# Scan stage: the order in which ScalarE's copy of u B reads PSUM and writes SBUF

## The reference, cut to what matters

```
dA  = exp(dt_t[:, :, None] * A)
hst = hst * dA + (dt_t * x_t)[:, :, None] * B_t[:, None, :]
y_t = einsum('bds,bs->bd', hst, C_t)
```

## Time and profile before

| what | us |
|---|---|
| median of three runs | 9105.0 |
| the profiled execution | 9109.74 |
| its span, first to last instruction | 9107.9 |
| stretch of the scan stage from the first to the last scan | 1341 to 6057 |
| VectorE busy in it (2048 scans) | 4616.65 |
| ScalarE busy in it | 4356.62 |
| TensorE busy in it | 4024.19 |

### The profile page before, as it was taken

One profiled execution on the slowest core, in us unless ns is written; L12 is line 12 of the kernel. 1 busy time (PEld: TensorE's weight loads), 2 busy tenths in 40 slices (PEclk: granted clock), 3 DMA queues, 4 the chain that ended last, 5 costly groups with the idle time before them and its releaser, 6 DMA issues. The chain is left out here.

```text
span 9107.9 us, 235238 instructions
## 1 busy us (share of the span) xinstructions
PE 7455.4 (82%) x94416; PEld 3961.6 (43%) x94416; DVE 6331.0 (70%) x5563; ACT 5948.1 (65%) x8010; POOL 1341.5 (15%) x799
## 2 busy tenths in 40 slices
PE   7677758888888888888888888877688888888888
PEld 4333324444444444444444444442244444344444
DVE  1332339999999999999999999963245344354554
ACT  1333339999999999999999999951135334343544
POOL 0000003222222222222222222310000000000000
PEclk8787769999899898889998999988899999999999
DMA  4444442222222222222222222223200000000000
GB/s 143 98 97 98 102 97 67 65 65 67 65 64 67 67 65 65 67 65 65 66 65 65 67 65 65 69 99 129 99 5 5 7 7 5 16 20 10 7 8 10
DMA packets 621391, 541.98 MB, mean 60 GB/s; under 512 B 490256, under 2 KB 528784, under 8 KB 606736
## 3 DMA queue, kind: packets, MB, share of 16 engines
q1 hardware_dynamic: 620320, 527.39, 19.8%
HBM read 381.77 MB, written 145.49 MB: 58 GB/s over the span
## 5 line engine op out<-in xcount | busy, mean ns | idle before, releaser
L1086 DVE TENSOR_TENSOR_SCAN s_h<-s_decay,s_h 128x1040 f32<-128x1040 f32 x2048 | 4616.6, 2323 | 132.2 <-ACT s_decay L1010 127.4
L981 ACT COPY s_h<-s_pb 128x1024 f32<-128x1024 f32 x2048 | 2514.3, 1228 | 190.9 <-PE s_pb L912 163.3
L925 PE MATMUL s_py<-s_h,s_cz 128*32 128x128 f32 x32768 | 2516.1, 437 | 1.7 <-DVE s_h L1086 1.7
L1010 ACT ACTIVATE s_decay<-s_pa 128x1024 f32<-128x1024 f32 x2048 | 2179.6, 1065 | 60.3 <-issue 55.0
L897 PE MATMUL s_pa<-s_dl,s_al 18*128 18x64 bf16 x32768 | 908.2, 198 | 666.9 <-ACT s_decay L1010 568.3
L925 PEld LDWEIGHTS s_py<-s_h,s_cz 128*32 128x32 f32 x32768 | 1056.3, 127 | 459.2 <-issue 4.7
L897 PEld LDWEIGHTS s_pa<-s_dl,s_al 18*128 18x128 bf16 x32768 | 660.7, 99 | 988.7 <-ACT s_decay L1010 912.8
L912 PEld LDWEIGHTS s_pb<-s_ul,s_bl 18*128 18x128 bf16 x16384 | 492.3, 97 | 1077.4 <-ACT s_h L981 866.1
L912 PE MATMUL s_pb<-s_ul,s_bl 18*128 18x128 bf16 x16384 | 867.6, 228 | 75.4 <-issue 59.1
L1053 POOL TENSOR_TENSOR s_h<-s_h,s_one 128x64 f32<-128x64 f32 x384 | 696.6, 1814 | 725.9 <-DVE s_h L1086 725.9
L1041 POOL TENSOR_TENSOR s_cz<-s_cl,s_one 128x128 f32<-128x128 f32 x256 | 320.4, 1252 | 2746.6 <-PE s_py L925 2734.3
(11 more groups left out here) (206 smaller groups left out, 6630.7 us busy)
## 6 DMA issues: line engine op xcount, KB each, us to landing
s_bl<-B SPq DMA_DIRECT2D x1024, 72.0 KB
s_ul<-U SPq DMA_DIRECT2D x1024, 72.0 KB
s_dl<-D SPq DMA_DIRECT2D x1024, 72.0 KB
s_al<-A SPq DMA_DIRECT2D x256, 144.0 KB
D<-p_dp SPq DMA_DIRECT2D x64, 384.0 KB, 6.5
U<-p_up SPq DMA_DIRECT2D x64, 384.0 KB, 5.3
B<-p_bz SPq DMA_DIRECT2D x144, 128.0 KB, 2.5
SZ<-p_sz SPq DMA_DIRECT2D x16, 1024.0 KB, 3.9
```

The costliest lines, as they stand in the source:

```text
L925: mm = pe.matmul(py[e % 2][QR * q:QR * q + QR, 0:P], cz[e % 2][:, l * P + QR * q:l * P + QR * q + QR], states, start=(l == 0), stop=(l == ...
L981: act.copy(out, pb[:].rearrange("p b t d -> p d b t")).then_inc(bu_done, 1)
L1010: act.activation(decay[(STEPS * e + 2 * z + j) % RING][:, :, 1:W], pa[j % 2][:], ACT.Exp).then_inc(exp_done, 1)
L1086: dve.tensor_tensor_scan(seg, decay[(STEPS * e + 2 * z + j) % RING][:].rearrange("p d w -> p (d w)"), seg, 0.0, ALU.mult, ALU.add).then_in ...
```

## The change

`take_bu` copies the same 1024 values of each partition from the same PSUM tile to the same places of `hb`, with the same waits and the same semaphore. Only the order in which it goes through them is another.

Before, the copy went channel by channel: for each of the 128 rows of `hb` it read 8 values of `pb`, each 128 values (512 bytes) behind the one before, and wrote them as two runs of 4 adjacent values. After, it goes time by time: for each of the 8 times it reads the 128 channels, which are adjacent in `pb`, and writes them one to a row, each 65 values (260 bytes) behind the one before.

```
-                    out = hb[at][:, :, 1:W].rearrange("p d (g a i) -> p d g a i", g=Q, i=4)[
-                        :, :, 2 * (h % 2):2 * (h % 2) + 2, h // 2, :]
-                    act.copy(out, pb[:].rearrange("p b t d -> p d b t")).then_inc(bu_done, 1)
+                    out = hb[at][:, :, 1:W].rearrange("p d (g a i) -> p g a i d", g=Q, i=4)[
+                        :, 2 * (h % 2):2 * (h % 2) + 2, h // 2]
+                    act.copy(out, pb[:]).then_inc(bu_done, 1)
```

## The result

The changed kernel takes 10,442.15 us (median of four runs, 10,438.45 to 10,451.34) against 9106.47 us: the ratio is 1.147, with a 95% interval of 1.145 to 1.149. It is 1336 us slower. The forecast was 950 us slower and a range up to 10,350 us. The direction and the new bound came out, the size did not. The profiled execution takes 10,442.36 us, its span is 10,440.6 us.

What follows compares the result with a forecast made beforehand. VectorE bounds the scan stage now; ScalarE at 2.70 us a step would make 21.9 us a tile, a stage of 5660 us against 4716 (+944), plus 6 for first copies: +950 on 9109.7, so 10,060 us, range 9020 to 10,350.

Steps and rivals of the forecast that it cites:

- the new bound: In the scan stage ScalarE, at 2.70 us a step, would replace VectorE, at 2.254 us a scan, as the bound.
- the reads are free: In the copy of `pb`, removing the separate PSUM reads would gain nothing; the old copy's 122 ns belonged to its writes.
- a value alone in its group of four: In the copy's writes to `hb`, each value alone in its aligned group of four costs 0.832 to 0.95 ns extra.
- L987 no longer waits: The small copy L987 would lose its 0.60 us wait for `ch` in each tile.
- The sign that the prediction had named for a wrong sum: First copies at 1.9 us while the scan stage still isn't near 5660 us.
- per step: ScalarE's step in the scan stage: copy slot 1.79 us plus exponential 0.91 us, 2.70 us, with TensorE done in time.
- The gaps at the loop's ends: ScalarE's gaps in front of exponentials that nothing released, 55.0 us at 17 places, would stay.
- the row for 0.95 ns a lone value: The old copy's 122 ns over 128 lone values, 0.95 ns each, would make the new copy 1.98 us.
- the round number of one slot: Each lone value in the copy costs one more slot of 0.832 ns, making the new copy 1.88 us.
- the clock in `ch`: TensorE's lower clock could show in `ch`; nothing was added for it, but the top of the range held it.
- reading (b): Copy's writes to `hb`: lone values in aligned groups of four cost extra; 10,060 us, own range 9900 to 10,350, chance 0.56.

Runs made afterwards that it cites:

- `ch_adj_after`: The changed kernel with TensorE's `ch` reading an adjacent 128-value tile instead of the states (y left out); 10,275 us.
- `bu_thin`: The changed kernel with `bu` making 2 of its 8 matmuls a step after the first tile; 10,418 us.
- `probe`: The kernel before, plus extra ScalarE and VectorE copies and memsets in many patterns, run in the quiet before the first tile; 9159.26 us.

## Why the prediction was wrong

Right were: the bound passes from VectorE to ScalarE in this stage; the reads are free; a value alone in its group of four is what costs; L987 no longer waits. The direction followed from these. The sign that the prediction had named for a wrong sum came: the first copies were near 1.9 us (1.97), and the stage took 6035 us and not 5660.

The step that failed is the term "per step": a slot of 1.79 us for the copy, 0.91 for the exponential, and nothing added for what TensorE does beside them. Per tile the mean distances of starts in the changed kernel's trace are 8 x 0.994 from an exponential to its copy, 6 x 1.900 + 1.967 + 1.894 for the copies, 0.178 + 0.212 for the small ones: 23.60 us, gaps included, against 21.9 + 0.2 in the forecast. By these slots the 375 us between 5660 and 6035 us of the stage come from:

- TensorE's single reads beside ScalarE's single writes: 1.878 instead of 1.79 us at 2040 copies, 180 us. The stage of `ch_adj_after` is 159 us shorter; of the other 20 us some 16 went into its exponentials' slots, since its `bu` took 0.61 us at every step. Rows 4 had a trace of it, since the slot there was 1.04 us and the first tiles' were 1.02. I did not compare the first two tiles with the later ones, and scaled nothing.
- The wait for `bu`: 1.041 instead of 0.968 us (means) at the 1113 exponentials with the long `bu`, 81 us. The prediction counted from the end of the exponential and found TensorE done. It left out that with a single `pb` the matmuls of `bu` start only when the copy before has ended. In the timeline above that is 0.31 us after the exponential began (4006.52 to 4006.83), and the next copy starts 0.11 us after `bu` has ended, so that 0.40 us fit beside the exponential and 0.61 us do not. The net gain of `bu_thin`, 21 us of the stage, is smaller, as said there.
- What the copy leaves to the instruction behind it: 0.047 us at 1535 exponentials, 72 us, and 0.178 + 0.212 - 0.31 = 0.08 us a tile at the small copies, 20 us. Its cause is argued, not shown.
- The copy in front of L987, 1.967 instead of 1.878 us: 22 us, cause open.
- The gaps at the loop's ends come to about the 55 us that the forecast had for them.

That the copy's slot without `ch` was 1.79 us, as forecast, is luck: two errors met. The copy alone took 1972 ns and not 1880 (`probe`), and it overlapped with what follows by 0.18 us and not by 0.09.

In the copy's price alone the row for 0.95 ns a lone value, which was in the working, would have given 1.98 us and been right. I chose the round number of one slot instead of the measured one. The first two items above were in no term. For the top of the range I had named the clock in `ch`; it was `bu` that the clock lengthened, and a contention beside it. The Trainium skill, "SBUF — State Buffer" (the note on cachelines in its section on the DMA port swizzle), on which the prediction drew for its reading (b), names lines of 16 bytes that need two hits each, and no step. The probe agrees with it in kind. One more slot for each value makes 1865 ns, which is what steps of 64 values measure and steps of 65 do not.

## What to carry to other kernels

A ScalarE copy that writes f32 to SBUF is priced first by how many values sit alone in an aligned group of four (none 1012 ns, all 1865 to 2076 ns in most steps tried), and then by the step between them (24 apart 2714 ns). Where the same values can be ordered either way, the long jumps belong on the PSUM side, where they cost ScalarE nothing. When an engine becomes the bound, an instruction's duration alone is not its slot: compare the same instruction in the quiet, in the first tiles and in the steady state, and take the last. An engine that writes into a single buffer can't start before the buffer is read, however far ahead it is otherwise. A wait of 0.6 us in front of the instruction that others need is worth moving behind it, even on an engine that is not the bound.

## What the runs showed of the hardware that I had not expected

- Copies of 1024 single values to SBUF, 24 apart, take ScalarE 2714 ns, two slots for each value more than adjacent ones; 64 apart they take 1865 ns, one slot more, and 65 apart 1972 ns. Pairs from offset 3, whose two values lie in two groups, cost as much as single values (1866 ns).
- Single reads from SBUF cost ScalarE about the same as single writes: 2008 ns for 1024 values 65 apart, against 1044 for adjacent ones. PSUM doesn't: 1012 ns at 1, 2, 32 and 128 values apart.
- VectorE pays for single writes in a copy (1990 against 1224 ns) and not in a memset (912 ns both).
- Single reads of TensorE lengthen ScalarE's copy of single values by 0.08 us of 1.8 us when they are 260 bytes apart, and by 0.12 us when they are 64 bytes apart in another tile. The copy of the kernel before, in runs of four, lost 0.03 us of 1.06 to them.
- A shorter `ch` with adjacent reads made the kernel before 1.2% slower: the granted clock went from 0.91 to 0.50, and `bu` and `adt` took 0.61 us instead of 0.40.
- GpSimd's carry (L1053) took 1814 ns beside back-to-back scans and 326 ns when VectorE had gaps, which suggests that its time in the first profile was mostly waiting.
